# A four-layer graph kernel on one core: the values by rows of the heads and of the output attention come from products of their own

## What is computed

```python
x = _layernorm(x + _L0_gnn_ref(x, W0, a0, adj))           # gated neighbour sums
x = _layernorm(x + _L1_gnn_ref(x, adj, Wh, bh, Wo, bo, gamma, beta))
x = _layernorm(x + _L2_gnn_ref(x, adj, W2, a2))           # additive attention
x = _layernorm(x + _L3_gnn_ref(x, adj, W3, a3))           # additive attention
```

```python
h = jnp.einsum('bnc,hdc->bhnd', x, Wh)                    # per head; D = 64
scores = jnp.where(mask, jnp.einsum('...nd,...md->...nm', h, h), NEG)
out_h = jnp.einsum('...nm,...md->...nd', softmax(scores), h) + b
z = leaky_relu(concat_of_heads(out_h), 0.2)               # 256 features
h2 = jnp.einsum('bnk,dk->bnd', z, Wo)                     # then the same with h2
```

## Time and profile before

| | |
|---|---|
| median of 3 executions | 6510.92 us (6500.03 to 6516.5) |
| profiled execution | 6511.56 us, span 6509.8 us |
| TensorE matmuls busy | 5744.7 us, 88% of the span |
| VectorE busy | 4424.1 us, 68% |
| ScalarE busy | 3901.8 us, 60% |
| GpSimd busy | 1599.2 us, 25% |
| mean granted TensorE clock | 0.942 of full speed |

### The profile page before, as it was taken

The page is one execution under the profiler, slowest core; times in us unless marked ns, Lnnn a source line. Parts: engine busy times, 40 slices in busy tenths (PEclk is TensorE's granted clock), DMA queues, the critical chain, the costliest instruction groups (busy, mean ns, idle before and its releaser), DMA issues.

```text
span 6509.8 us, 163090 instructions
## 1 busy us (share of the span) xinstructions
PE 5744.7 (88%) x52064; PEld 4654.5 (71%) x52064; DVE 4424.1 (68%) x7928; ACT 3901.8 (60%) x5701; POOL 1599.2 (25%) x1239
## 2 busy tenths in 40 slices
PE   7689898998989888998989989898889989899866
PEld 4268676886768777786768867687777867688655
DVE  4756476766766676766767667766767677676765
ACT  1056457666666656666576666666566675766655
POOL 0100014023230413104140231304131041402354
PEclk9889899999999999999989999999999999899988
DMA  4200000000000000000000000000000000000000
GB/s 137 64 5 2 1 5 2 2 2 9 5 2 2 2 11 2 2 2 4 10 2 2 2 9 5 2 2 3 11 2 2 2 4 9 2 2 2 8 1 4
DMA packets 99234, 55.58 MB, mean 9 GB/s; under 512 B 89424, under 2 KB 92752, under 8 KB 98384
## 3 DMA queue, kind: packets, MB, share of 16 engines
q1 hardware_dynamic: 60496, 34.71, 1.9%
q10 hardware_dynamic: 37888, 9.97, 0.7%
HBM read 35.75 MB, written 8.91 MB: 7 GB/s over the span
## 4 chain that ended last, share of the span: by engine, by line
PE 67%; issue 9%; DVE 9%; ACT 5%; DVEq 3%; POOL 1%; ACTq 0%; DMA 0%; SPq 0%; POOLq 0%
PE tp L878 23%; PE po L898 23%; PE pss L869 7%; PE pss L868 7%; DVE rows L1172 3%; DVEq L237 3%; ACT pss L1039 2%; DVE pt L1184 2%; ACT rows L1060 2%; PE px L829 2%; PE px L825 1%; PE tp L887 1%; PE px L843 1%; PE px L835 1%; DVE tmp L254 1%
## 5 line engine op out<-in xcount | busy, mean ns | idle before, releaser
L878 PE MATMUL tp<-ident,rows 128*128 128x128 f32 x14336 | 2054.5, 285 | 181.6 <-DVE pt L1184 89.7
L1184 DVE COPY pt<-tp 128x512 f32<-128x512 f32 x2048 | 1336.5, 686 | 1287.7 <-PE tp L878 1272.5
L878 PEld LDWEIGHTS tp<-ident,rows 128*128 128x128 f32 x14336 | 1609.7, 144 | 592.0 <-issue 554.9
L1060 ACT ACTIVATE rows<-rows,nm 128x2048 f32<-128x2048 f32 x896 | 1797.5, 2006 | 265.4 <-DVE nm L1172 257.5
L898 PE MATMUL po<-pt,hn 128*64 128x128 f32 x28672 | 1887.0, 288 | 0.5 <-DVE pt L1184 0.2
L898 PEld LDWEIGHTS po<-pt,hn 128*64 128x64 f32 x28672 | 1667.8, 145 | 164.7 <-issue 164.7
L707 POOL TENSOR_TENSOR rows<-sr,mask 128x2048 f32<-128x2048 f32 x256 | 1046.4, 4088 | 697.3 <-PE tp L878 679.2
L1012 ACT COPY pt<-tp 128x512 f32<-128x512 f32 x1536 | 850.7, 589 | 449.1 <-PE tp L878 429.2
L868 PE MATMUL pss<-ha 128*128 128x512 f32 x2560 | 1067.8, 417 | 24.6 <-issue 15.3
L869 PE MATMUL pss<-ha,hb 128*128 128x512 f32 x2560 | 1015.3, 397 | 0.0
L1172 DVE CUSTOM_DVE_ANT_0 rows<-pss,mask,nm 128x1024 f32<-128x1024 f32 x640 | 821.7, 1284 | 202.6 <-issue 201.4
(11 more groups left out here) (102 smaller groups left out, 3375.0 us busy)
## 6 DMA issues: line engine op xcount, KB each, us to landing
adjb<-in_adj SPq DMA_DIRECT2D x32, 512.0 KB, 4.6
xin<-x SPq DMA_DIRECT2D x9, 512.0 KB, 4.2
xb<-in_x ACTq DMA_DIRECT2D x16, 256.0 KB, 3.4
x<-t ACTq DMA_DIRECT2D x16, 256.0 KB, 2.7
xb<-x SPq DMA_DIRECT2D x8, 512.0 KB, 4.2
out<-xb SPq DMA_DIRECT2D x32, 128.0 KB, 2.0
xtp<-in_xt SPq DMA_DIRECT2D x12, 256.0 KB, 6.6
ab<-in_a ACTq DMA_DIRECT2D x16, 64.0 KB, 3.3
```

The source lines that it names most:

```text
L878: last = nc.tensor.transpose(tp[row.bank[q]][:, r * P:(r + 1) * P], rows[:, row.slot, jb * P:(jb + 1) * P], ident[:])
L1060: nc.scalar.activation(rows[:, row.slot, :], rows[:, row.slot, :], ACT.Exp, scale=-1.0, bias=nm[:, row.t, 1:2], accum_out=rs[:, row.t:row. ...
L1184: nc.vector.tensor_copy(pt[:, CH * q:CH * (q + 1), row.k % SLOTS, :], tp[row.bank[q]][:].rearrange("p (j n) -> p j n", n=P)).then_inc(pt_d ...
```

## The change

The third copy of every `proj` task is left out. The values by rows are computed instead of transposed: for a head, four products of a block of `xt` (as weights, 64 partitions by 128 columns) with the head's 64 columns of `wh`; for the output attention, four times two accumulating products of a block of `zt` with `wo`.

```diff
@@ attention_layers @@
-        hf = whf[D:P, :]
@@ block.tensor, run_task @@
                 elif name == "hn":
                     px_free()
                     for q in range(CH):
-                        last = nc.tensor.transpose(px[:, q * D:(q + 1) * D], hf[:, q * P:(q + 1) * P],
-                                                   ident[D:P, D:P])
+                        own, block = px[:, q * D:(q + 1) * D], slice(q * P, (q + 1) * P)
+                        if unit == GAT2:
+                            for k in range(2):
+                                last = nc.tensor.matmul(own, zt[:, c % 2, k, block], wo[:, k, 0:D],
+                                                        start=(k == 0), stop=(k == 1))
+                        else:
+                            last = nc.tensor.matmul(own, xt[:, cols][:, block], wh[:, unit, 0:D],
+                                                    start=True, stop=True)
                     last.then_inc(hn_psum, 1)
                     px_used(hn_c)
@@ block.scalar, run_task @@
                     nc.scalar.copy(ha[i][0:D, cols], px[0:D, :])
-                    nc.scalar.copy(hb[i][D:P, cols], px[D:P, :])
-                    nc.scalar.copy(hf, px[D:P, :]).then_inc(h1_ready, 1)
+                    nc.scalar.copy(hb[i][D:P, cols], px[D:P, :]).then_inc(h1_ready, 1)
```

## The result

The changed kernel takes 6615.27 us (median of 4 executions, 6612.96 to 6625.9) against 6509.9 us for the kernel before: a ratio of 1.0154, 95% interval 1.0133 to 1.0174. It is slower by 105 us; the profiled execution's span grew from 6509.8 to 6611.2 us, by 101.4. The forecast was 6606 us, 95 above, and slower.

What follows compares the result with a forecast made beforehand. TensorE was taken to set the pace in heads 1 and 2, with waits back and forth with ScalarE in the additive layers. 57 + 16 + 25 - 14 + 11 = +95 us gave 6606 us, range 6555 to 6650.

Steps and rivals of the forecast that it cites:

- The price of a product: From L843's run: 1.04 us against 0.39 per head chunk, +0.65 us; +1.6 us per output chunk, at full clock.
- TensorE sets the pace: Second layer, heads 1 and 2, prologue's heads: 96 head chunks at 0.65 us, 62 us, less 5 for idle time: +57.
- Second layer and head 0: TensorE's idle time there could swallow all 18 us of 28 chunks; only 5 us was taken off.
- The covered output chunks: Second additive layer, two per pass: TensorE's wait for an exponential hides the added 1.6 us; taken as 0, at most 22.
- The second additive layer: 28 output chunks there: together +25 us, range 22 to 70, before any gain from the removed copies.
- two exposed chunks: Second additive layer, per pass, in the chain at low clock: 1.6 to 3.4 us each, taken as 1.8; 25 us in all.
- first additive layer: 28 head chunks, one in four hidden by a wait, the others 0.65 us or 0.8 at low clock: +16 us.
- The copy: Removed ScalarE copies in the additive layers: half of 27 us gained, -14 us, range -27 to 0.
- The serial chunks: Prologue, 4 head and 4 output chunks in series: dearer products less the 0.49 us copy each, +11 us.
- Rival 3: Additive layers: the clock stays up, saving 140 us in all, so the kernel ends at about 6466 us; chance 0.05.
- rival 2: The low clock costs its full price: +174 at most, +150 with half the covered output chunks exposed, 6660 us; chance 0.08.

Runs made afterwards that it cites:

- e6: The changed kernel with every head's product issued twice into the same place: 6735.24 us, ratio 1.0344 to the kernel before.
- filled pair: The kernel before and the changed kernel, each with 12 unread identity transposes ahead of each turning back in the additive layers: 6330.2 and 6408.21 us.
- e2: The kernel before without the third copy, its transposes reading the rounded values in hb instead: 6503.16 us, ratio 0.9976.
- e4: The change for the heads alone; the output attention keeps the transposes and copy of the kernel before: 6588.77 us, ratio 1.0101.
- e1: The changed kernel with the third copy of every proj task put back, where nobody reads it: 6657.87 us, ratio 1.0213 to the kernel before.
- e9: The changed kernel with 12 unread identity transposes ahead of each turning back in the additive layers: 6408.21 us, ratio 0.9832 to the kernel before.
- e10: The kernel before with 12 unread identity transposes ahead of each turning back in the additive layers: 6330.2 us, ratio 0.9719.
- e7: The kernel of e5 with 12 unread identity transposes ahead of each turning back in the additive layers: 6305.08 us, ratio 0.9685 to the kernel before.
- e5: The kernel before without the third copy, values by rows from one product per block of ha with two stacked identities: 6507.85 us, ratio 0.9981.

## Why the prediction was right, point by point

**The price of a product** was read from L843's row, and it held: two records each, 1.03 us for the run of eight against 1.04 assumed. The rule of four passes in the Trainium skill ("FP8 and Floating Point Precision", TensorE Precision Notes), read as in the prediction, would have made the run four times the transposes, an estimate of 1.56 us; the chain shows 2.6 times. That doesn't refute the rule: inside the runs a product's two records take 0.22 us and a transpose 0.06, 3.6 times, and the steps at a run's two ends, 0.1 to 0.2 us, are much the same in both kernels.

**TensorE sets the pace** in the stages of heads 1 and 2 and in the prologue's heads: 37.8 + 7.2 = 45.0 us for 68 chunks, 0.66 each, forecast 0.65. Shown also by e6, up to the low clock that appeared in head 1.

**Second layer and head 0** was mis-sized. I took off 5 of 18 us for slack and got +4.5 in all; e6 and the filled pair (+12.6) show that 0.16 to 0.45 us a chunk remain there. Two reasons are in the trace. The transposes had small waits beside them that the products now fill: two in four per pass took 0.49 and 0.60 us to the start of the turns, where the products take 1.00. And head 1's first chunk, reckoned with the additive layer, falls into head 0's last row by these borders: run and wait behind it took 2.43 us and take 1.94, in e2 as well, so there the removed copy's 0.49 us come back whole, 3.4 us in all. The rest of the missing 8.5 us is open.

**The covered output chunks** cost nothing, as taken: behind the third and fourth chunk of each pass TensorE had waited 1.59 to 1.69 us (the earlier trace rows show the one case of 1.30), so run and wait took 2.1 us; now the run takes 1.73 us to the start of the turns, without a wait behind it.

```profile
1520.88 1.90 PE L837 MATMUL px<-wo,xz 128*128 128x64 f32 x16
1522.61 1.04 PE L883 MATMUL tp<-ident,rows 128*128 128x128 f32 x8
```

**The second additive layer** is the term of the sum that failed in size: +18 forecast with its share of the copies, +33.3 measured. In the first pass the two exposed chunks take 3.49 and 3.46 us in the chain, so the instructions themselves do run at the low clock that I had reckoned to be repaid. Over the seven passes the 14 runs last 3.3 us on average (2.0 to 3.7) where the transposes lasted 0.7: 2.6 us more each where I had taken 1.8, some 37 us instead of 25. The first pass:

```profile
1476.90 3.49 PE px L837 x16
1480.39 1.71 PE tp L883 x8
...
1494.36 3.46 PE px L837 x16
```

In the filled pair the whole stage grows by 7.5 us, so some 26 of the 33 us came with the low clock in these profiled executions; by the medians of both pairs it is 27 us for the whole kernel. My step, that longer products at the low clock "would rather take over slow time from what follows than add to it", was wrong as a rule. In the first additive layer it did no harm: the exposed runs grew by 0.83 us on average to the start of the turns, near the 0.75 taken. e4's 18 us in the second, with no changed instruction there, may mean that a stage can lose clock by what is changed before it, or be the difference between two executions; no run here settles that.

**The copy** alone gave 16 us (forecast 18 with the prologue's part), and that it came so near was partly luck: I had put half of the copies' time into each additive layer, and e2's stages show 18.3 us back in the first and 13.7 lost in the second. That the copy is worth some 38 beside the products was not foreseen; the additive layers' clock is where the difference shows, but e1 changes ScalarE's work and the clock together, so that cause is argued and not shown.

**The serial chunks** came at 12.5 us for 11.

**The rivals.** Rival 3 had the right resource and the wrong trigger: products instead of transposes don't hold the clock, work in TensorE's idle time does, and it is worth more than the 140 us that I gave it (183 to 203). In rival 2's sum the middle value was wrong: with half of the covered chunks exposed, 11 of their 22 us, +174 becomes +163 and not +150. Two errors of +15 and -9 us cancelled in part, so that 95 was nearer to the measured 101 to 105 than its parts were.

## What to carry to other kernels

A transpose that is replaced by an f32 product trades one record for two; where TensorE sets the pace that is paid in full (0.65 us a chunk here), while a copy taken from an engine beside it pays little (16 us for 160 copies here). Price a new instruction by the row of the nearest shape that is already there, stage by stage, and by the length of its run in the chain, not by the spacing of its records alone. And where an engine waits at a lowered clock, look at the clock first: here filling an idle wait with work that nobody reads was worth more than anything in the change.

## What the runs showed of the hardware that was not expected

- Twelve transposes that nobody reads in each of TensorE's waits for ScalarE's copy held the granted clock of the additive layers at 1.00 (0.98 in one pass each of e9 and e10), instead of 0.85 to 0.90, and the kernel gained 2.8% (e10) to 3.0% (e7 against e5). Transposes and products did it alike (6305 and 6302 us); four instead of twelve gave a fifth of it (6464).
- A stage's clock differs without a change in the stage: in the kernel before the second additive layer took 115.5 us at 0.90 in some passes and 120.5 us at 0.87 in others, and in e4 121.8 us at 0.86, with the same instructions.
- A one-record product of 128 partitions with 64 moving columns comes 0.11 us apart (e5), as each record of the two-record products of 64 partitions does; the transposes of 64 partitions with 64 moving columns came 0.06 us apart. A run of four of these products with the eight turns behind it still took less of the chain than one of four transposes, 1.30 us against 1.41.
